# One comparison for the one-hots of two quads, its column numbers read from PSUM

## The reference

```python
h  = relu(layernorm(x))
xp = h @ lin1_w
C  = 0.5 * (cos(edge_weight * pi / 10) + 1)
W  = (ssp(edge_attr @ mlp_w1 + mlp_b1) @ mlp_w2 + mlp_b2) * C[:, None]   # ssp = softplus - ln 2
agg = segment_sum(xp[src] * W, dst, num_segments=12500)
out = x + ssp(agg @ lin2_w + lin2_b) @ lin_w + lin_b
```

## Time and profile before

| | |
|---|---|
| median of 3 runs | 2082.06 us (2080.72 to 2082.11) |
| the profiled execution's own time | 2083.55 us |
| its span, first to last instruction | 2081.7 us |
| POOL, busy | 1567.1 us (75%) |
| PE, busy | 1294.3 us (62%) |
| DVE, busy | 1087.0 us (52%) |
| ACT, busy | 897.4 us (43%) |
| granted TensorE clock over the span, of full speed | 0.814 |

### The profile page before, as it was taken

The page is one execution under the profiler, slowest core; times in us unless marked ns, Lnnn a source line. Parts: engine busy times, 40 slices in busy tenths (PEclk is TensorE's granted clock), DMA queues, the critical chain, the costliest instruction groups (busy, mean ns, idle before and its releaser), DMA issues.

```text
span 2081.7 us, 46568 instructions
## 1 busy us (share of the span) xinstructions
PE 1294.3 (62%) x12671; PEld 1104.4 (53%) x12879; DVE 1087.0 (52%) x3570; ACT 897.4 (43%) x1536; POOL 1567.1 (75%) x1641
## 2 busy tenths in 40 slices
PE   6577756566656566656666565656556556566565
PEld 5465645555545555555555554545545455455454
DVE  8778646555545554454444444545445444444444
ACT  5675544444435444433344343334343343344332
POOL 7777777777777777777777777777777777777775
PEclk9798978888878778787788788888887787887778
DMA  8632333333333333333333333232332332323321
GB/s 311 229 93 75 85 88 78 89 81 78 88 88 78 88 89 83 83 83 76 88 88 84 83 88 88 71 88 75 83 88 70 88 87 71 88 74 83 88 71 48
DMA packets 115664, 190.15 MB, mean 91 GB/s; under 512 B 33428, under 2 KB 63096, under 8 KB 115276
## 3 DMA queue, kind: packets, MB, share of 16 engines
q0 software_dynamic: 52352, 107.32, 20.7%
q1 hardware_dynamic: 63052, 79.84, 13.0%
HBM read 174.23 MB, written 12.80 MB: 90 GB/s over the span
## 4 chain that ended last, share of the span: by engine, by line
POOL 42%; issue 21%; SPq 21%; PE 6%; DMA 4%; DVE 4%; ACT 2%; DVEq 0%; POOLq 0%; ACTq 0%
POOL XG L410 42%; SPq L370 15%; SPq L366 5%; DMA XG<-xp_scratch,IX 3%; PE PW L741 2%; PE PA L755 1%; DVE XG L638 1%; SPq L314 1%; ACT XG L432 1%; PE PX L685 1%; DVE TB L530 1%; DVE SCR L509 1%; PE PX L724 1%; PE PW L697 1%; PE PW L738 1%
## 5 line engine op out<-in xcount | busy, mean ns | idle before, releaser
L410 POOL DMA_INDIRECT XG<-xp_scratch,IX x1572 | 1503.6, 957 | 479.3 <-issue 469.6
L638 DVE SCALAR_TENSOR_TENSOR XG<-PW,CC,XG 128x128 f32<-128x128 f32 x1636 | 459.8, 343 | 582.0 <-DMA XG<-xp_scratch,IX 582.0
L476 ACT ACTIVATE TB<-PX 128x512 f32<-128x512 f32 x416 | 243.8, 586 | 1045.1 <-PE PX L724 1043.9
L741 PE MATMUL PW<-W,TB 128*128 128x128 f32 x3322 | 542.9, 317 | 120.0 <-DVE XG L638 86.7
L741 PEld LDWEIGHTS PW<-W,TB 128*128 128x128 f32 x3322 | 542.9, 232 | 20.0
L738 PEld LDWEIGHTS PW<-BPB,ones 128*128 128x128 bf16 x416 | 41.7, 100 | 655.4 <-issue 647.8
L738 PE MATMUL PW<-BPB,ones 128*128 128x512 bf16 (+1 forms) x209 | 97.9, 468 | 463.9 <-DVE XG L638 460.9
L724 PE MATMUL PX<-AT,W 51*128 51x256 f32 x1662 | 284.0, 468 | 139.1 <-DMA AT<-attr_t 135.4
L605 DVE SCALAR_TENSOR_TENSOR TB<-PX,TB 128x512 f32<-128x512 f32 x416 | 282.7, 680 | 165.9 <-ACT TB L480 164.5
L480 ACT ACTIVATE TB<-TB,HALF 128x512 f32<-128x512 f32 x416 | 299.8, 721 | 13.5
L755 PE MATMUL PA<-OH,XG 128*64 128x64 f32 x6528 | 293.0, 257 | 0.0
(11 more groups left out here) (82 smaller groups left out, 513.1 us busy)
## 6 DMA issues: line engine op xcount, KB each, us to landing
HT<-xp_scratch SPq DMA_DIRECT2D x3092, 0.5 KB
AT<-attr_t SPq DMA_DIRECT2D x206, 200.0 KB
XG<-xp_scratch,IX POOLq DMA_INDIRECT x1572
AG<-zero SPq DMA_DIRECT2D x1, 6400.0 KB, 22.6
xp_scratch<-XG SPq DMA_DIRECT2D x24, 256.0 KB, 2.6
XR<-x SPq DMA_DIRECT2D x24, 256.0 KB, 4.4
out<-XR SPq DMA_DIRECT2D x24, 256.0 KB, 2.6
AG<-x SPq DMA_DIRECT2D x11, 512.0 KB, 10.2
```

The lines of the kernel that those rows point to most:

```text
L410: e.indirect_dma_start(XG[q % XG_N][0:p, k * D:(k + 1) * D], None, xp, bass.IndirectOffsetOnAxis(ap=IX[0:p, t0 + k:t0 + k + 1], axis=0)).t ...
L476: e.activation(T[:, 0:w], PX[q % X1_N][:, 0:w], ACT.Abs).then_inc(s_ab, 1)
L638: ins = e.scalar_tensor_tensor(out=G, in0=PW[q % 2][0:p, k * D:(k + 1) * D], scalar=CC[0:p, t0 + k:t0 + k + 1], in1=G, op0=ALU.mult, op1=A ...
L741: ins = e.matmul(P[0:p, k * D:(k + 1) * D], TB[q % TB_N][:, k * TILE:k * TILE + p], W2[:, :], start=False, stop=(k == n - 1), skip_group_c ...
```

## The change

The constant `WP` is a third stretch of 64 columns in the bank PA; the column numbers are copied there once, ahead of the main loop and behind a wait for the prelude's last use of the bank. The comparison then reads its column numbers from WP (PSUM) in place of WI (SBUF), and REL from SBUF as before. One comparison serves two quads: 8 tiles by 64 columns, 512 elements per partition, in place of two of 256. It stands at VectorE's step q + 2 of the even quad, behind the adds of a pair, in place of steps q + 3 and q + 4. There are two buffers of a pair each in place of six of a quad each, and there is no wait of its own for a free buffer: the adds in front of it at the same step wait for the scatters of the pair before last. Only for the last pair, which has a full quad and a single tile of 20 edges, two comparisons are made. TensorE's wait on `s_oh` and its read of OH follow.

```diff
-    XG_N, TB_N, X1_N, OH_N = 26, 4, 4, 6
+    XG_N, TB_N, X1_N, OH_N = 26, 4, 4, 2
-        OH = [sb(f"OH{i}", [128, QT, WIN]) for i in range(OH_N)]
+        OH = [sb(f"OH{i}", [128, 2 * QT, WIN]) for i in range(OH_N)]
+        WP = PA[:, 2 * WIN:3 * WIN]
+        def onehots(q):
+            t0 = q * QT
+            n = min(2 * QT, EDGES // TILE - t0)
+            return [(0, t0, n, TILE)] + ([(n, t0 + n, 1, EDGES % TILE)] if n < 2 * QT and EDGES % TILE else [])
...
+            e.wait_ge(s_xe, NPC)
+            link(e.tensor_copy(WP, WI[:, 0:WIN]))
...
-                q = i - 3
-                if 0 <= q < NQ:
-                    t0, n, last = quad(q)
-                    if q >= OH_N:
-                        e.wait_ge(s_sc, q - OH_N + 1)
-                    p = last if n == 1 else TILE
-                    assert n == 1 or last == TILE
-                    e.tensor_tensor(OH[q % OH_N][0:p, 0:n, :], WI[0:p, 0:WIN].unsqueeze(1).to_broadcast([p, n, WIN]),
-                                    REL[0:p, t0:t0 + n].unsqueeze(2).to_broadcast([p, n, WIN]),
-                                    ALU.is_equal).then_inc(s_oh, 1)
+                q = i - 2
+                if q % 2 == 0 and 0 <= q < NQ:
+                    for o, t0, n, p in onehots(q):
+                        ins = e.tensor_tensor(OH[q // 2 % OH_N][0:p, o:o + n, :],
+                                              WP[0:p, :].unsqueeze(1).to_broadcast([p, n, WIN]),
+                                              REL[0:p, t0:t0 + n].unsqueeze(2).to_broadcast([p, n, WIN]), ALU.is_equal)
+                    ins.then_inc(s_oh, 1)
...
-                    e.wait_ge(s_oh, q + 1)
+                    e.wait_ge(s_oh, q // 2 + 1)
...
-                                           OH[q % OH_N][0:p, k, :], start=(k == 0), stop=(k == n - 1))
+                                           OH[q // 2 % OH_N][0:p, q % 2 * QT + k, :], start=(k == 0), stop=(k == n - 1))
```

More of the change, by code:

```diff
@@ L256, in gnn_kernel @@
         P3 = xp[0:FULL, :].rearrange("(p t) d -> p t d", p=TILE)
-        half = [OH[i][:, :, :].rearrange("p k w -> p (k w)").bitcast(bf16).rearrange("p (k i d) -> p k i d", k=2, i=2)
+        half = [OH[i][:, 0:QT, :].rearrange("p k w -> p (k w)").bitcast(bf16).rearrange("p (k i d) -> p k i d", k=2, i=2)
                 for i in range(2)]
```

## The result

| | kernel before | changed kernel |
|---|---|---|
| median of 4 runs each | 2082.09 us (2080.72 to 2084.39) | 2068.73 us (2068.01 to 2071.65) |
| ratio | | 0.9937, 95% interval 0.992 to 0.9955 |
| the profiled execution's own time | 2083.55 us | 2071.65 us |
| its span | 2081.7 us | 2069.9 us |

The change saves 13.4 us by the medians, 13.1 by the ratio; I had forecast 16.1. Two later comparisons of the same two kernels, on other chips, both gave 0.9936 (0.9922 to 0.9949).

What follows compares the result with a forecast made beforehand. POOL's pitch of back-to-back gathers was taken to bound the kernel. Span: 2081.7 - 16.0 - 0.14 = 2065.6 us; against the median, 2082.06 - 16.1 = 2066 us, 0.8% faster, range 2063 to 2069.5.

Steps and rivals of the forecast that it cites:

- The bound and the cause: POOL's gather pitch alone sets the time; L623, with both inputs in SBUF, holds up gathers that start within it.
- The value of zero: Gathers starting in the new comparison, with column numbers in PSUM, have zero excess, as those in L590 and L605.
- The first rival: Comparison still holds gathers, and longer, because REL is in the way; 30.0 us of excess, 2096 us; chance 0.06.
- The term of 16.0 us: Excess over 0.944 us of 114 gathers starting inside L623, removed from POOL's path; hits may be 10% off.
- My own formula: Hits are hold over pitch, each costing half the hold; 13.9 us for the kernel before, scaled by 1.15.
- The first refill: POOL's gather of quad 26 at 137.47 us needs quad 0's scatter; no wait expected, at most 0.5 us lost once.
- The margin of 0.6 us: Time left between quad 0's scatter and quad 26's gather; claimed to stay, L638 of quads 0 and 1 starting 0.3 earlier.
- The end: Chain of 13.3 us after the last gather; 0.14 us go with the 20-row comparison that stands in it.
- 32 us less of VectorE: One comparison per pair saves VectorE 0.15 us each in 208 pairs; worth nothing, as VectorE waits for gathers.
- the copy into PSUM: Copy of 64 elements ahead of the loop, at most 0.2 us, covered by VectorE's idle time before the first L605.
- no wait for buffers OH: The moved wait: adds already wait for the same scatters, so dropping the wait for a free OH buffer costs nothing.
- idle time per gather 0.305: Sign of a right prediction: POOL's idle time, almost all issue, stays unchanged at 0.305 us per gather.

Runs made afterwards that it cites:

- e_two_from_psum: Changed kernel with two comparisons of 256 elements, one per quad, both from PSUM, in place of the pair's one; 0.9934 of the kernel before.
- e_pair_from_sbuf: Changed kernel with its one comparison of 512 elements reading the column numbers from WI in SBUF; 1.0076 of the kernel before, 2101.92 against 2087.29 us.
- f_two_from_sbuf: Changed kernel with two comparisons of 256 elements from SBUF, back to back at the changed kernel's place; 0.9989 of the kernel before.
- f_after_again: Changed kernel once more, nothing altered, beside the kernel before; 0.9936, 2068.99 against 2083.25 us.
- f_halves_from_sbuf: Kernel before with each comparison cut in two of 128 elements, from SBUF, in the old place; 0.9977 of the kernel before.
- e_before_again: Kernel before once more, nothing altered; 0.9998, 2086.5 us against 2087.29 beside it.
- e_after_again: Changed kernel once more, nothing altered, on another chip than its first measurement; 0.9936 of the kernel before, 2073.11 against 2087.29 us.

## Why the prediction was right, and where its sizes were off

*The bound and the cause.* Right, and shown: with the column numbers in PSUM no gather is held (e_two_from_psum, the changed kernel three times), with them in SBUF they are (e_pair_from_sbuf), at the length that the elements give. Neither the merging (e_two_from_psum against the changed kernel: 0.9934 and 0.9936) nor the place (f_two_from_sbuf: 0.9989) carries the gain. The value of zero for a gather that starts in the new comparison holds. The first rival is refuted for the change: REL is read from SBUF as a broadcast in every version, and without WI beside it holds nothing. Its price came true where both were in SBUF: 30.0 us of excess forecast, 29.0 measured.

*The rule on ports.* By the Trainium skill's page "SBUF — State Buffer" (section "Who interferes with whom") a VectorE instruction with two SBUF inputs contends with a GpSimd instruction that reads SBUF, and the loser is blocked until the other has ended. That two SBUF inputs contend is what the runs show, and of the instructions with one, that those with the other input in PSUM don't; the flags' cast with its one SBUF input does. That the loser waits until the instruction has ended they don't show, and the measurement counts: at 512 elements the comparison lasts 0.68 us and the gather gets on at 0.56, at 128 it is 0.28 and 0.16. The missing 0.12 us is the same at each length.

*The term of 16.0 us* was mis-sized as a forecast, though not as a reading: it belongs to one execution, and the next one had 13.5. I had allowed 10% and it is 16%. My own formula gave 13.9, and I scaled it up by 1.15 to agree with the one count; unscaled it would have forecast 2082.06 - 13.9 - 0.14 = 2068.0, where 2068.73 was measured. I also set the sum against the profiled execution and then moved it to the median by a constant 1.5 us, without asking whether that execution was slow because of its hits. From the mean of the two, 14.8, the forecast would have been 2067. The measured median lies 2.7 us above the forecast and 0.8 below the upper end of the range, and the profiled execution (2071.65) beyond it.

*The first refill.* The margin of 0.6 us was read rightly, and the claim that it stays was wrong in its reason. I left out that step 4 has the next pair's comparison in front of quad 1's L638. The scatter of quad 0 ends 9.75 us behind the loop's first L605 in the kernel before (136.90 - 127.15, by the sixteenth matmul of L755) and 9.98 in the changed one (135.88 - 125.90, f_after_again), so it is 0.2 us later and not 0.3 earlier. That is small beside what differs between executions. From the end of quad 0's scatter to the refill's gather it is 0.57 us in the profile that I predicted from, and 1.5 to 5.1 us in the seven later ones with 26 buffers in which POOL didn't wait. The start of the loop lies between 123.7 and 129.7 us over ten profiles, and in the first of the changed kernel it was late by enough for a wait of 2.5 us. I had bounded the loss at 0.5, for the change alone.

*The end.* I gave -0.14 us. The comparison in it did go: the 20-row L645 starts 0.13 us behind the last add's start (2059.57 and 2059.70) where it had been 0.27. But the stretch got longer, 13.25 to 14.75 us, and the records show where most of it lies: the scatter of quads 412 and 413.

```profile
2070.28 1.16 PE L755 MATMUL PA<-OH,XG 128*64 128x64 f32 x32
```

```profile
2057.01 1.98 PE L762 MATMUL PA<-OH,XG 128*64 128x64 f32 x32
```

The granted clock over the 3 us from there is 0.95 before (2070 to 2073) and 0.56 after (2057 to 2060), that is mostly 2.4 GHz and mostly 1.2:

```profile
2070.00:2073.00 3.00, 2.41 (x54) 1.76 (x52) 2.30 (x9) 0.00 (x0) 0.00 (x0) 0.95 0.30 87
```

```profile
2057.00:2060.00 3.00, 2.82 (x49) 2.64 (x48) 1.87 (x8) 0.00 (x0) 0.00 (x0) 0.56 0.32 88
```

Over the ten profiles on chips of the usual speed, with the granted clock from the end of the last gather to the end of the span:

| place of the comparisons | granted clock | the end, us |
|---|---|---|
| old (before, f_halves_from_sbuf) | 0.76 | 13.25, 13.35 |
| old (e_before_again) | 0.62 | 14.15 |
| new (e_two_from_psum) | 0.76 | 13.83 |
| new (six others) | 0.62 | 14.38 to 14.78 |

```profile
2070.63:2084.78 14.15, 6.36 (x68) 4.35 (x67) 4.35 (x15) 0.85 (x2) 0.00 (x1) 0.62 0.12 32
```

```profile
2053.20:2067.03 13.83, 4.47 (x63) 3.14 (x63) 4.32 (x14) 0.85 (x2) 0.00 (x1) 0.76 0.12 33
```

So two things add up. At a clock of 0.62 in place of 0.76 the end is 0.8 to 0.9 us longer, in either place; and at the same clock it is some 0.5 us longer with the pair's place. The first happened with the unchanged kernel too, so the change isn't needed for it; whether it makes it likelier (six of seven against one of three) is not settled. The second rests on three profiles of the old place, and its cause is open.

*The account.* The mean end is 13.6 us in the old place and 14.5 in the new one, 0.9 more. 14.8 us of holds less 0.9 at the end is 13.9; measured are 13.1 to 13.4, within an interval of 3.6 us to each side. The wait at the first refill belongs to the one profile, and so to the run of 2071.65 us, not to the median.

*The rest* went as forecast: L629 at 0.68 us 209 times, 32 us less of VectorE worth nothing, the copy into PSUM (0.23 us) hidden in front of the first L615, no wait for buffers OH, idle time per gather 0.305.

## What to carry to other kernels

Where GpSimd issues gathers back to back, look at the distribution of their durations and at what VectorE runs when the long ones start; the mean less the median times the count is what there is to win. What counts is not how busy VectorE is but how long its single instructions with two SBUF inputs are (a long cast or tensor_scalar from SBUF is one to look at too): the loss to each grows with the square of its length, so either put one input into PSUM, or cut the instruction into pieces, and don't merge two of them into a longer one. Of the two cures the first was worth 13 us here and the second 5. Before a gain from one profile is forecast, work out the hits from the hold and the pitch, or count them in a second execution.

## What was not expected of the hardware

The undisturbed gather lasted 0.9435 us on the average in most profiles and 0.946 in four of fourteen (3.7 us over the kernel), with nothing in the program to tell them apart; e_before_again and e_pair_from_sbuf are two of them, on one chip. On that chip the profiled executions of e_after_again and e_two_from_psum had 0.9435 and were 2.6 and 3.7 us faster than the next of their kernel. That the others had 0.946 would fit, but they were not traced. And one chip ran the kernel before in 2965 us where the others needed 2079 to 2089, with SP's queue and not POOL setting the pace.
